# Projecting q, k and v of a first attention by halves, in three passes

## The chip, the cores and the metric

The kernel runs on one core of a Trainium2 chip. The metric is the device time of one execution in microseconds (us), lower is better. The profile is of one execution on the chip; its times are in us, those marked ns in nanoseconds. TensorE is PE in its rows (PEld are its weight loads), VectorE is DVE, ScalarE is ACT, GpSimd is POOL and SyncE is SP.

## The reference

Two transformer layers act on x of shape (4, 256, 256), 1,024 tokens in all. Each layer is an attention and a feed-forward part, each behind a layer norm with a shift and scale per batch. The change touches the first attention alone, which has 16 heads of 128 channels:

```python
q = _silu(x @ Wq)          # x: 1024 tokens x 256; each W: 256 x 2048
k = _silu(x @ Wk)
v = _silu(x @ Wv)
z = x @ Wz
```

q, k and v then pass a causal convolution of four taps along the sequence, q and k a rotary embedding and a norm; each token attends to itself and the three before it; the result is gated with silu(z), scaled and projected back to 256 columns. The later parts are a feed-forward layer whose weights are looked up in a table of 16 values, a second, full attention and a mixture of 32 experts.

## The kernel before

Everything is one hand-ordered program: each engine has its own instruction list, and semaphores order them. `project` multiplies one head's weights (two blocks of 128 x 128) with the 1,024 tokens of `h_t` in plain fp32; the profile shows each fp32 matmul as two records. The second attention uses `by_halves` instead: an operand is split into an upper part, rounded to the fp32r type by a copy, and a lower part, the rest; three single-pass products (lower times upper, upper times lower, upper times upper) add up in PSUM.

The first attention runs in turns, one per head. Turn h projects q, k, v and z of head h (work marked 1), finishes the attention of head h - 1 (marked 2) and transposes the gated result of head h - 2 (marked 3). `turns0` writes out turns 0, 1, 16 and 17 and loops over the pairs between; every engine runs the same turns with its own function `turn`. In one turn the engines do, each strictly in this order:

- TensorE: q; transpose of `rows_sb`; transposes of the gated result; k; S, the banded scores; v; z; transposes of v; sums of squares (`ssq`); the attention output o.
- ScalarE: silu and first tap of q; the copy into G; silu and first tap of k; the same of v; squares of q and k; silu of z; `v_tok`; the gate's tanh; squares of o (`sqo`).
- VectorE: gate mask `gm`; the other three taps of q's convolution (L1090); `ssq_s`; k's taps; the product A; cosine and sine parts (L1096, L1102); v's taps; the copy of the sums into `rows_sb` (L1139); the gate product `a0_g` (L1150).
- GpSimd: the norm's power, and the DMAs that add the rotary halves.
- SyncE: loads `b_all`, and the head after next's weights once z is done; it also fills two DRAM buffers for the experts.

The weights of a head lie in `wh[par]`, two buffers for even and odd heads. The table indices of the feed-forward part are loaded at the very start into `lut_w`; they are first used after the last turn.

Of the kernel before, what the change touches and what calls it, by code (L numbers as in the profile page):

```python
# [5 lines left out]
ALU = mybir.AluOpType  # L6
# [7 lines left out]
P = 128  # L14
# [45 lines left out]
def build(nc, a, out, b_rows, code_rows):  # L60
# [41 lines left out]
    with ctx:  # L102
# [42 lines left out]
        def carve(*sizes, base=0, of=arena):  # L145
# [8 lines left out]
        (uq, uk, uv, cq, ck, cv0, cv1, swq, swk, qr, kr, sqq, sqk, sz0, sz1, gm, A, v_tok, junk,  # L154
         rows_sb, gate, b_all, wh0, wh1) = carve(
            UW, UW, UW, T, T, T, T, T, T, T + PAD, T, T, T, T, T, BAND, BAND, T, T,
# [3 lines left out]
        cv, sz, wh = [cv0, cv1], [sz0, sz1], [wh0, wh1]  # L160
        wmod = [G[:, 0:KC * 6 * D], G[:, KC * 6 * D:2 * KC * 6 * D]]
# [6 lines left out]
        (wout,) = carve(H * D, base=3 * UW + 14 * T + PAD + 2 * BAND + P)  # L168
# [168 lines left out]
        def turns0(eng, turn):  # L337
            turn(0, 0, 0, (1,))
            turn(1, 0, 1, (1, 2))
            with eng.Fori(1, H // 2) as i:  # L340
                turn(2 * i, i, 0, (1, 2, 3))
                turn(2 * i + 1, i, 1, (1, 2, 3))
            turn(H, H // 2, 0, (2, 3))
            turn(H + 1, H // 2, 1, (3,))
# [18 lines left out]
        def _(sp):  # L363
# [8 lines left out]
            for par in range(2):  # L372
                sp.dma_start(wh[par], a["w_qkvz"][par]).then_inc(sg(f"a0_w{par}"), 16)
            sp.dma_start(lut_idx[:, 0:LPRE], a["idx_pre"]).then_inc(sg("in_idx"), 16)
            sp.dma_start(lut_idx[:, LPRE:LUTC - LPOST].rearrange("p (h c) -> p h c", c=LW),
                         a["idx"].rearrange("h p c -> p h c")).then_inc(sg("in_idx"), 16)
            sp.dma_start(lut_idx[:, LUTC - LPOST:LUTC], a["idx_post"]).then_inc(sg("in_idx"), 16)
# [24 lines left out]
            sp.wait_ge(sg("a0_z"), H)  # L402
            sp.wait_ge(sg("a0_gm"), H)
# [64 lines left out]
        def _(pe):  # L468
# [48 lines left out]
            def turn(h, hh, par, st):  # L517
                def w(j, k):
                    return wh[par][:, (j * KC + k) * P:(j * KC + k) * P + P]

                if 1 in st:
                    pe.wait_ge(sg(f"a0_w{par}"), 16 * (hh + 1))
# [4 lines left out]
                    project(slot(0), lambda k: w(0, k), P).then_inc(sg("a0_q"), 1)  # L527
# [13 lines left out]
                if 1 in st:  # L541
# [5 lines left out]
                    project(slot(1), lambda k: w(1, k), P).then_inc(sg("a0_k"), 1)  # L547
# [10 lines left out]
                if 1 in st:  # L558
                    pe.wait_ge(sg("a0_silu_q"), h + 1)
                    project(slot(0), lambda k: w(2, k), P).then_inc(sg("a0_v"), 1)  # L560
# [38 lines left out]

            turns0(pe, turn)  # L600
# [130 lines left out]
            pe.wait_ge(sg("in_lo"), KC)  # L731
# [112 lines left out]
        def _(act):  # L844
# [6 lines left out]

            def turn(h, hh, par, st):
# [30 lines left out]
                if 1 in st:  # L883
                    silu_and_tap(1, "k", ck)
                    silu_and_tap(2, "v", cv[par])
# [717 lines left out]
```

## Time and profile before

| what | us |
|---|---|
| median of 3 runs | 1256.71 |
| lowest and highest | 1248.58, 1257.54 |
| the profiled execution's own time | 1249.32 |
| its span | 1247.5 |
| TensorE busy in the span | 1091.8 (88%) |
| VectorE busy | 759.9 (61%) |
| ScalarE busy | 554.3 (44%) |
| GpSimd busy | 264.9 (21%) |

Busy time is a share of the whole span and averages over stages with different limits. In a stretch view each engine has its busy time with the count of its records; behind them stand the clock that was granted to TensorE (1.00 is 2.4 GHz, 0.50 is 1.2 GHz) and the DMA engines' share. A timeline row gives start and duration of a run of like instructions; what stands in brackets is how long the engine had idled before it and what released it. Records of a matmul overlap, so the pitch from start to start tells what one costs.

### The profile page before, as it was taken

The page shows a single profiled execution, that of the slowest core. Times are in us where ns is not written, and L with a number is a line of the kernel's source. Part 1 is how long each engine was busy: PE and PEld are TensorE (multiplying, and loading weights), DVE is VectorE, ACT ScalarE, POOL GpSimd, SP SyncE. Part 2 cuts the span into 40 slices and gives each one's busy share as a digit, 9 for nine tenths or more (in the row PEclk, how much of TensorE's full clock was granted, in tenths as well). Part 3 has the DMA queues.
Part 4 walks back from the last instruction along what each step waited for, and adds up shares of the span by engine and source line. Part 5 has one row for each costly group of instructions (what it writes and reads, how often), then busy time and mean ns, then how long its engine had stood idle before and what let it go on. Part 6 is the DMA issues. An engine that isn't in the chain of part 4 may idle for free.

```text
span 1247.5 us, 16995 instructions
## 1 busy us (share of the span) xinstructions
PE 1091.8 (88%) x5693; PEld 779.3 (62%) x5693; DVE 759.9 (61%) x1332; ACT 554.3 (44%) x1256; POOL 264.9 (21%) x228
## 2 busy tenths in 40 slices
PE   6989999999999979947977999999998967329996
PEld 4666667666766664423436999988985425128885
DVE  1497788878887858963136778787772034303344
ACT  1266767676766648920014555655551002002320
POOL 0032223222222220012002111111100000546660
PEclk9799999999999978978988999999998987759997
DMA  6055445643555330060001110111001000148854
GB/s 266 19 143 138 100 95 140 129 110 95 128 132 145 78 101 1 1 185 1 0 0 52 52 50 26 50 50 50 25 0 51 1 13 1 76 161 262 271 170 178
DMA packets 51349, 110.50 MB, mean 89 GB/s; under 512 B 7827, under 2 KB 30558, under 8 KB 50544
## 3 DMA queue, kind: packets, MB, share of 16 engines
q1 hardware_dynamic: 41584, 84.32, 20.9%
q0 software_dynamic: 9728, 25.72, 10.4%
q8 instruction: 20, 0.33, 0.1%
q14 instruction: 17, 0.14, 0.0%
HBM read 69.52 MB, written 27.89 MB: 78 GB/s over the span
## 4 chain that ended last, share of the span: by engine, by line
PE 41%; DVE 12%; issue 4%; POOL 3%; ACT 2%; DMA 1%; DVEq 0%; POOLq 0%; ACTq 0%; SPq 0%
PE psum L709 5%; PE psum L611 4%; PE psum L797 4%; PE psum L512 4%; PE psum L490 3%; PE psum L492 3%; PE psum L491 3%; PE psum L682 3%; PE psum L807 2%; DVE arena L1197 2%; POOL slot_rows L1514 2%; PE psum L628 2%; PE psum L249 1%; DVE lut_w L1197 1%; PE psum L786 1%
## 5 line engine op out<-in xcount | busy, mean ns | idle before, releaser
L1090 DVE SCALAR_TENSOR_TENSOR arena<-arena,par_in 128x1024 f32<-128x1024 f32 x144 | 184.7, 1284 | 52.5 <-ACT arena L870 38.3
L512 PE MATMUL psum<-h_t,arena 128*128 128x512 f32 x384 | 174.0, 597 | 0.0
L512 PEld LDWEIGHTS psum<-h_t,arena 128*128 128x128 f32 x384 | 69.3, 190 | 73.2 <-issue 73.2
L611 PE MATMUL psum<-G,arena 128*128 128x512 f32 x256 | 112.6, 602 | 2.7 <-DVE G L1289 1.5
L961 ACT ACTIVATE arena<-psum,small 128x256 f32<-128x256 f32 x128 | 59.2, 472 | 85.8 <-DVE small L1237 85.7
L611 PEld LDWEIGHTS psum<-G,arena 128*128 128x128 f32 x256 | 49.3, 193 | 64.8 <-issue 64.8
L1469 POOL TENSOR_TENSOR small<-small 128x16 f32<-128x16 f32 x16 | 46.8, 2928 | 199.5 <-DVE small L1116 199.5
L860 ACT ACTIVATE arena<-psum 128x1024 f32<-128x1024 f32 x48 | 49.3, 1026 | 83.4 <-PE psum L512 83.4
L490 PE MATMUL psum<-arena_r 128*128 128x256 f32 x256 | 77.7, 303 | 1.5 <-DVE arena_r L1262 1.5
L1475 POOL DMA_DIRECT2D arena<-arena x64 | 53.9, 983 | 117.4 <-DVE arena L1102 117.2
L286 POOL TENSOR_TENSOR small<-small 128x8 f32<-128x8 f32 x6 | 9.9, 1642 | 321.7 <-DVE small L277 305.7
L491 PE MATMUL psum<-arena_r 128*128 128x256 f32 x256 | 73.3, 286 | 0.0
L492 PE MATMUL psum<-arena_r 128*128 128x256 f32 x256 | 73.3, 286 | 0.0
L1522 POOL DMA_INDIRECT out_rows<-arena x64 | 62.7, 980 | 46.2 <-DVE arena L1382 24.0
L1491 POOL TENSOR_TENSOR arena_r<-arena,arena_r 128x512 fp32r<-128x512 f32 x16 | 21.2, 1325 | 217.0 <-ACT arena_r L972 217.0
L565 PEld LDWEIGHTS psum<-arena,h_t 128*128 128x128 f32 x512 | 59.7, 192 | 7.7 <-issue 7.7
L922 ACT ACTIVATE arena<-psum,small 128x128 f32<-128x128 f32 x128 | 44.9, 377 | 42.7 <-PE psum L596 42.7
L709 PE MATMUL psum<-arena,h_t 128*128 128x128 f32 x512 | 62.2, 275 | 0.0
L709 PEld LDWEIGHTS psum<-arena,h_t 128*128 128x128 f32 x512 | 60.7, 192 | 1.5 <-DVE arena_r L1255 0.2
L797 PE MATMUL psum<-arena 128*128 128x256 f32 x256 | 61.3, 383 | 0.0
L490 PE MATMUL psum<-lut_w_r,arena_r 128*128 128x512 f32 x128 | 51.4, 402 | 10.1 <-POOL arena_r L1491 10.1
L565 PE MATMUL psum<-arena,h_t 128*128 128x128 f32 x512 | 59.7, 274 | 0.0
(194 smaller groups left out, 2357.2 us busy)
## 6 DMA issues: line engine op xcount, KB each, us to landing
arena<-arena POOLq DMA_DIRECT2D x64, 256.0 KB, 7.6
arena<-in_w_moe SPq DMA_DIRECT2D x32, 384.0 KB, 3.8
slot_rows<-nowhere SPq DMA_DIRECT2D x16, 576.0 KB, 4.9
arena<-slot_rows SPq DMA_DIRECT2D x32, 288.0 KB, 3.9
arena<-in_w_qkvz SPq DMA_DIRECT2D x16, 512.0 KB, 3.8
arena<-b_rows SPq DMA_DIRECT2D x16, 512.0 KB, 9.0
arena<-in_qkv_codes SPq DMA_DIRECT2D x16, 384.0 KB, 3.2
arena<-in_qkv_scales SPq DMA_DIRECT2D x64, 96.0 KB, 3.0
```

Source lines behind the costliest of these rows:

```text
L490: nc.tensor.matmul(dst, w_l, x_h, start=start, stop=False, skip_group_check=True)
L491: nc.tensor.matmul(dst, w_h, x_l, start=False, stop=False, skip_group_check=True)
L492: return nc.tensor.matmul(dst, w_h, x_h, start=False, stop=stop, skip_group_check=True)
L512: i = nc.tensor.matmul(dst[0:rows, n * 512:n * 512 + 512], w(k), h_t[:, k * T + n * 512:k * T + n * 512 + 512], start=(k == 0), stop=(k == ...
L565: i = nc.tensor.matmul(slot(1)[:, t * P:t * P + P], h_t[:, k * T + t * P:k * T + t * P + P], w(3, k), start=(k == 0), stop=(k == KC - 1))
L611: i = nc.tensor.matmul(bank(2 * m + n), w[:, h * D + m * P:h * D + m * P + P], G[:, h * T + n * 512:h * T + n * 512 + 512], start=(h == 0) ...
L709: i = nc.tensor.matmul(slot(0)[:, t * P:t * P + P], h_t[:, k * T + t * P:k * T + t * P + P], w(2, k), start=(k == 0), stop=(k == KC - 1))
L797: i = nc.tensor.matmul(bank(2 + 2 * (e % 2) + j)[:, 0:CAP], we[e % WRING][:, k * D + j * P:k * D + j * P + P], xT[e % 2][:, k * CAP:(k + 1 ...
L961: e = nc.scalar.activation(prob[b % 2][:, i * S:i * S + S], bank(4 + b % 2)[:, i * S:i * S + S], ACT.Exp, bias=nmax[:, 2 * b + i:2 * b + i ...
L1090: nc.vector.scalar_tensor_tensor(by_batch(dst), by_batch(u[s])[:, :, j:j + S], par_in[:, bass.ds(M_CW + (w * H + h) * TAPS + j, 1)], by_ba ...
L1475: nc.gpsimd.dma_start(rot[s][to:to + 64, :], sw[s][of:of + 64, :], accum_op=ALU.add)\
L1522: nc.gpsimd.indirect_dma_start(out_rows, bass.IndirectOffsetOnAxis(place.bitcast(I32)[:, c:c + 1], 0), eo[e % RING][:, r * D:(r + 1) * D], ...
```

## The change

The q, k and v projections of the first attention go by halves; z stays fp32. The tokens are split once ahead of the first turn (`hh_h` by ScalarE, `hh_l` by VectorE, both laid over `lut_w`). Each head's q, k and v weights are split one turn ahead: ScalarE's `upper0` behind k's tap copies the upper part into `w_hi`, VectorE's `lower0` behind the copy of `rows_sb` writes the rest over the fp32 weights in place. `turns0` gets a mark 4 for that work, and turns 14 and 15 are now written out. The squares of o go into `v_tok` instead of a buffer of their own, which is dropped to make room, and the table indices are loaded behind the last z projection instead of at the start.

```diff
--- before.py
+++ after.py
@@ -151,13 +151,16 @@
             return v
 
         UW = B * (S + PAD)
-        (uq, uk, uv, cq, ck, cv0, cv1, swq, swk, qr, kr, sqq, sqk, sz0, sz1, gm, A, v_tok, junk,
+        (uq, uk, uv, cq, ck, cv0, cv1, swq, swk, qr, kr, sqq, sqk, sz0, sz1, gm, A, v_tok,
          rows_sb, gate, b_all, wh0, wh1) = carve(
-            UW, UW, UW, T, T, T, T, T, T, T + PAD, T, T, T, T, T, BAND, BAND, T, T,
+            UW, UW, UW, T, T, T, T, T, T, T + PAD, T, T, T, T, T, BAND, BAND, T,
             P, BAND, T, 4 * KC * P, 4 * KC * P)
         u, c_ = {"q": uq, "k": uk, "v": uv}, {"q": cq, "k": ck}
         sw, rot, sqr = {"q": swq, "k": swk}, {"q": qr[:, 0:T], "k": kr}, {"q": sqq, "k": sqk}
         cv, sz, wh = [cv0, cv1], [sz0, sz1], [wh0, wh1]
+        at_w = 3 * UW + 13 * T + PAD + 2 * BAND + P + BAND + T
+        wl0, _, wl1, _, w_hi0, w_hi1 = carve(QKV, KC * P, QKV, KC * P, QKV, QKV, base=at_w, of=arena_r)
+        w_lo, w_hi = [wl0, wl1], [w_hi0, w_hi1]
         wmod = [G[:, 0:KC * 6 * D], G[:, KC * 6 * D:2 * KC * 6 * D]]
         ba_sb = G[0:2 * H, 2 * KC * 6 * D:2 * KC * 6 * D + T]
 
@@ -165,7 +168,7 @@
         ln_c, ln_sq, ln_b, rb, gsb, hsb0, hsb1, lv0, lv1, lb0, lb1 = carve(
             KC * T, KC * T, T, T, T, T, T, (PAIRS - 1) * LC, (PAIRS - 1) * LC, LC, LC)
         lut_v, lut_b0 = [lv0, lv1], [lb0.bitcast(I32), lb1.bitcast(I32)]
-        (wout,) = carve(H * D, base=3 * UW + 14 * T + PAD + 2 * BAND + P)
+        (wout,) = carve(H * D, base=3 * UW + 13 * T + PAD + 2 * BAND + P)
         hsb = [hsb0, hsb1]
 
         QK = 2 * KC * P
@@ -335,11 +338,13 @@
 
 
         def turns0(eng, turn):
-            turn(0, 0, 0, (1,))
-            turn(1, 0, 1, (1, 2))
-            with eng.Fori(1, H // 2) as i:
-                turn(2 * i, i, 0, (1, 2, 3))
-                turn(2 * i + 1, i, 1, (1, 2, 3))
+            turn(0, 0, 0, (1, 4))
+            turn(1, 0, 1, (1, 2, 4))
+            with eng.Fori(1, H // 2 - 1) as i:
+                turn(2 * i, i, 0, (1, 2, 3, 4))
+                turn(2 * i + 1, i, 1, (1, 2, 3, 4))
+            turn(H - 2, H // 2 - 1, 0, (1, 2, 3, 4))
+            turn(H - 1, H // 2 - 1, 1, (1, 2, 3))
             turn(H, H // 2, 0, (2, 3))
             turn(H + 1, H // 2, 1, (3,))
 
@@ -371,10 +376,6 @@
             sp.dma_start(lut, a["lut"].broadcast_to([P, LUT])).then_inc(sg("in_lut"), 16)
             for par in range(2):
                 sp.dma_start(wh[par], a["w_qkvz"][par]).then_inc(sg(f"a0_w{par}"), 16)
-            sp.dma_start(lut_idx[:, 0:LPRE], a["idx_pre"]).then_inc(sg("in_idx"), 16)
-            sp.dma_start(lut_idx[:, LPRE:LUTC - LPOST].rearrange("p (h c) -> p h c", c=LW),
-                         a["idx"].rearrange("h p c -> p h c")).then_inc(sg("in_idx"), 16)
-            sp.dma_start(lut_idx[:, LUTC - LPOST:LUTC], a["idx_post"]).then_inc(sg("in_idx"), 16)
             sp.wait_ge(sg("ba_sb"), 1)
             sp.dma_start(b_rows, ba_sb[0:H, :]).then_inc(sg("b_rows"), 16)
             sp.wait_ge(sg("b_rows"), 16)
@@ -400,6 +401,10 @@
             turn(H - 2, H // 2 - 1, 0, False)
             turn(H - 1, H // 2 - 1, 1, False)
             sp.wait_ge(sg("a0_z"), H)
+            sp.dma_start(lut_idx[:, 0:LPRE], a["idx_pre"]).then_inc(sg("in_idx"), 16)
+            sp.dma_start(lut_idx[:, LPRE:LUTC - LPOST].rearrange("p (h c) -> p h c", c=LW),
+                         a["idx"].rearrange("h p c -> p h c")).then_inc(sg("in_idx"), 16)
+            sp.dma_start(lut_idx[:, LUTC - LPOST:LUTC], a["idx_post"]).then_inc(sg("in_idx"), 16)
             sp.wait_ge(sg("a0_gm"), H)
             sp.dma_start(wout, a["w_out"]).then_inc(sg("in_wout"), 16)
 
@@ -518,13 +523,21 @@
                 def w(j, k):
                     return wh[par][:, (j * KC + k) * P:(j * KC + k) * P + P]
 
-                if 1 in st:
-                    pe.wait_ge(sg(f"a0_w{par}"), 16 * (hh + 1))
+                def project0(dst, j):
+                    for n in range(2):
+                        for k in range(KC):
+                            w, c = slice((j * KC + k) * P, (j * KC + k) * P + P), slice(k * T + n * 512, k * T + n * 512 + 512)
+                            i = by_halves(dst[:, n * 512:n * 512 + 512], w_hi[par][:, w], w_lo[par][:, w], hh_h[:, c], hh_l[:, c],
+                                          k == 0, k == KC - 1)
+                    return i
+
+                if 1 in st:
+                    pe.wait_ge(sg("a0_w_lo"), h + 1)
                     if since(h, 1):
                         pe.wait_ge(sg("a0_silu_v"), h)
                     if since(h, 2):
                         pe.wait_ge(sg("a0_v_tok"), h - 1)
-                    project(slot(0), lambda k: w(0, k), P).then_inc(sg("a0_q"), 1)
+                    project0(slot(0), 0).then_inc(sg("a0_q"), 1)
                 if 2 in st:
 
                     pe.wait_ge(sg("a0_rows_sb"), h)
@@ -544,7 +557,7 @@
                     if since(h, 2):
                         pe.wait_ge(sg("a0_g"), h - 1)
                         pe.wait_ge(sg("a0_sqo"), h - 1)
-                    project(slot(1), lambda k: w(1, k), P).then_inc(sg("a0_k"), 1)
+                    project0(slot(1), 1).then_inc(sg("a0_k"), 1)
                 if 2 in st:
 
                     pe.wait_ge(sg("a0_rope_q"), 32 * h)
@@ -557,7 +570,7 @@
                     m.then_inc(sg("a0_S"), 1)
                 if 1 in st:
                     pe.wait_ge(sg("a0_silu_q"), h + 1)
-                    project(slot(0), lambda k: w(2, k), P).then_inc(sg("a0_v"), 1)
+                    project0(slot(0), 2).then_inc(sg("a0_v"), 1)
                 if 1 in st:
                     pe.wait_ge(sg("a0_silu_k"), h + 1)
                     for t in range(NT):
@@ -597,6 +610,7 @@
                                                  stop=True, skip_group_check=True)
                     m.then_inc(sg("a0_o"), 1)
 
+            pe.wait_ge(sg("in_lo"), KC)
             turns0(pe, turn)
 
             pe.wait_ge(sg("in_wout"), 16)
...
@@ -849,6 +863,12 @@
             act.wait_ge(sg("ba_ps"), 1)
             nc.scalar.activation(ba_sb, psum[0:2 * H, 4 * 512:4 * 512 + T], ACT.Copy).then_inc(sg("ba_sb"), 1)
 
+            def upper0(h, hh, par):
+                act.wait_ge(sg(f"a0_w{par}"), 16 * (hh + 1))
+                if since(h, 2):
+                    act.wait_ge(sg("a0_v"), h - 1)
+                nc.scalar.activation(w_hi[par], wh[par][:, 0:QKV], ACT.Copy).then_inc(sg("a0_w_hi"), 1)
+
             def turn(h, hh, par, st):
                 def cw(w, j):
                     return par_in[:, bass.ds(M_CW + (w * H + h) * TAPS + j, 1)]
@@ -882,6 +902,9 @@
                                          scale=par_in[:, bass.ds(M_NW + h - 2, 1)]).then_inc(sg("a0_gT_sb"), 1)
                 if 1 in st:
                     silu_and_tap(1, "k", ck)
+                if 4 in st:
+                    upper0(h + 1, hh + par, 1 - par)
+                if 1 in st:
                     silu_and_tap(2, "v", cv[par])
                     for s in "qk":
                         act.wait_ge(sg("a0_conv_" + s), 3 * h + 3)
@@ -895,7 +918,7 @@
                 if 2 in st:
                     act.wait_ge(sg("a0_vT"), h)
                     if since(h, 2):
-                        act.wait_ge(sg("a0_o"), h - 1)
+                        act.wait_ge(sg("a0_sqo"), h - 1)
                     act.wait_ge(sg("a0_rqk"), h)
                     for i in range(NT):
                         c = slice(i * P, i * P + P)
@@ -919,10 +942,14 @@
                         if i == NT // 2:
                             m.then_inc(sg("a0_sqo_lo"), 1)
                             act.wait_ge(sg("a0_g_hi"), h)
-                        m = nc.scalar.activation(junk[:, i * P:i * P + P], slot(1)[:, i * P:i * P + P], ACT.Square, scale=rqk[1 - par][:, i:i + 1],
+                        m = nc.scalar.activation(v_tok[:, i * P:i * P + P], slot(1)[:, i * P:i * P + P], ACT.Square, scale=rqk[1 - par][:, i:i + 1],
                                                  accum_out=ss_all[:, bass.ds((h - 1) * NT + i, 1)])
                     m.then_inc(sg("a0_sqo"), 1)
 
+            for k in range(KC):
+                act.wait_ge(*norm("n0", "out", k))
+                nc.scalar.activation(chunk(hh_h, k), chunk(h_t, k), ACT.Copy).then_inc(sg("in_hi"), 1)
+            upper0(0, 0, 0)
             turns0(act, turn)
             for c in range(LCH):
                 o, n = lut_cols(c)
@@ -1080,6 +1107,17 @@
                                     0.5, None, ALU.mult)\
                 .then_inc(sg("a_sb"), 1)
             dve.wait_ge(sg("in_par"), 16)
+            for k in range(KC):
+                dve.wait_ge(sg("in_hi"), k + 1)
+                nc.vector.tensor_tensor(chunk(hh_l, k), chunk(h_t, k), chunk(hh_h, k).bitcast(F32), ALU.subtract)\
+                    .then_inc(sg("in_lo"), 1)
+
+            def lower0(h, par):
+                dve.wait_ge(sg("a0_w_hi"), h + 1)
+                nc.vector.tensor_tensor(w_lo[par], wh[par][:, 0:QKV], w_hi[par].bitcast(F32), ALU.subtract)\
+                    .then_inc(sg("a0_w_lo"), 1)
+
+            lower0(0, 0)
 
             def turn(h, hh, par, st):
                 def conv(w, s, dst):
@@ -1137,6 +1175,8 @@
                     if since(h, 1):
                         dve.wait_ge(sg("a0_ssqT"), h)
                     nc.vector.tensor_copy(rows_sb[0:2 * NT, :], bank(7)[0:2 * NT, 0:P]).then_inc(sg("a0_rows_sb"), 1)
+                if 4 in st:
+                    lower0(h + 1, 1 - par)
                 if 2 in st:
 
                     dve.wait_ge(sg("a0_o"), h)
...
```

On VectorE, in the loop's first turn, the order before stood so between the last sine part and the next turn's gate mask (names in brackets are semaphores waited for; `ISA` rows set addresses in registers):

```order
L1102 TENSOR_TENSOR arena<-arena,cst 128x1024 [waits a0_rope_k]
L1090 ISA [waits a0_tap_v]
L1090 SCALAR_TENSOR_TENSOR arena<-arena,par_in 128x1024
L1090 ISA [waits a0_conv_v]
L1090 SCALAR_TENSOR_TENSOR arena<-arena,par_in 128x1024
L1090 ISA [waits a0_conv_v]
L1090 SCALAR_TENSOR_TENSOR arena<-arena,par_in 128x1024
L1139 COPY arena<-psum 16x128 [waits a0_ssqT,a0_ssq]
L1150 SCALAR_TENSOR_TENSOR arena<-psum,small,arena 128x128 [waits a0_silu_z,a0_o]
L1150 SCALAR_TENSOR_TENSOR arena<-psum,small,arena 128x128 x3
```

The same engine and place in the changed kernel (L1117 is `lower0`, L1177 the copy of `rows_sb`, L1190 the gate product):

```order
L1128 SCALAR_TENSOR_TENSOR arena<-arena,par_in 128x1024
L1177 COPY arena<-psum 16x128 [waits a0_ssqT,a0_ssq]
L1116 REGISTER_ALU
L1117 TENSOR_TENSOR arena_r<-arena,arena_r 128x768 [waits a0_w_hi]
L1190 SCALAR_TENSOR_TENSOR arena<-psum,small,arena 128x128 [waits a0_silu_z,a0_o]
L1190 SCALAR_TENSOR_TENSOR arena<-psum,small,arena 128x128 x3
```

One subtraction of 768 columns has come in between the copy and the gate product; nothing else on VectorE changed places inside a turn.

On TensorE, between the attention output of one turn (L592, L596) and the q projection of the next (L512), before:

```order
L592 MATMUL psum<-arena 128x128 x2
L596 MATMUL psum<-arena 3x128
L512 MATMUL psum<-h_t,arena 128x512 [waits a0_v_tok,a0_silu_v,a0_w1]
L512 MATMUL psum<-h_t,arena 128x512 x3
L533 MATMUL psum<-cst,arena 128x128 [waits a0_ssq_s,a0_rows_sb]
```

And in the changed kernel (L605, L609 are the attention output; L495 to L497 the three products of `by_halves`, which repeat to twelve):

```order
L605 MATMUL psum<-arena 128x128 x2
L609 MATMUL psum<-arena 3x128
L535 REGISTER_ALU
L495 MATMUL psum<-lut_w_r,arena_r 128x512 [waits a0_v_tok,a0_silu_v,a0_w_lo]
L496 MATMUL psum<-lut_w_r,arena_r 128x512
L497 MATMUL psum<-lut_w_r,arena_r 128x512
```

The order of the products among TensorE's other work is the same; the q projection now waits for the semaphore of `lower0` where it waited for the weights' DMA.

## Rows read from the trace of the kernel before

**Rows 1.** Stretches, by engine: busy us (count); then granted clock, DMA share, GB/s.

```profile
95.13:422.30 327.17, 327.17 (x1887) 223.44 (x1886) 271.90 (x338) 229.02 (x546) 81.66 (x65) 1.00 0.49 117
...
220.96:246.13 25.17, 25.17 (x146) 17.19 (x146) 20.91 (x26) 17.62 (x42) 6.28 (x5) 1.00 0.50 117
```

**Rows 2.** Timeline, turn 7: start us, us, engine, line, operation, idle before.

```profile
220.96 3.70 PE L512 MATMUL psum<-h_t,arena 128*128 128x512 f32 x8
...
224.78 1.03 ACT L860 ACTIVATE arena<-psum 128x1024 f32<-128x1024 f32 x1 [0.70 <-PE psum L512]
...
227.27 1.29 DVE L1090 SCALAR_TENSOR_TENSOR arena<-arena,par_in 128x1024 f32<-128x1024 f32 x1 [2.27 <-ACT arena L870]
...
230.29 1.15 ACT L870 ACTIVATE arena<-arena,par_in 128x1024 f32<-128x1024 f32 x1
...
231.61 4.14 DVE L1090 SCALAR_TENSOR_TENSOR arena<-arena,par_in 128x1024 f32<-128x1024 f32 x3
...
234.35 1.03 ACT L860 ACTIVATE arena<-psum 128x1024 f32<-128x1024 f32 x1 [2.92 <-PE psum L512]
...
245.49 0.27 DVE L1139 COPY arena<-psum 16x128 f32<-16x128 f32 x1
```

**Rows 3.** Timeline of TensorE: single by-halves matmuls of the second attention.

```profile
662.67 0.63 PE L492 MATMUL psum<-lut_w_r,arena_r 128*128 128x512 f32 x1
...
663.95 0.63 PE L492 MATMUL psum<-lut_w_r,arena_r 128*128 128x512 f32 x1
...
750.27 0.40 PE L490 MATMUL psum<-lut_w_r,arena_r 128*128 128x512 f32 x1
...
752.14 0.39 PE L492 MATMUL psum<-lut_w_r,arena_r 128*128 128x512 f32 x1
```

**Rows 4.** By form, VectorE and ScalarE, early second attention: count | busy, mean ns.

```profile
L1262 DVE TENSOR_TENSOR arena_r<-psum,arena_r 128x512 fp32r<-128x512 f32 x5 | 3.3, 683 | 0.0
...
L1225 DVE TENSOR_TENSOR lut_w_r<-h_t,lut_w_r 128x1024 fp32r<-128x1024 f32 x2 | 2.4, 1222 | 0.0
...
L998 ACT ACTIVATE lut_w_r<-h_t 128x1024 fp32r<-128x1024 f32 x2 | 2.1, 1058 | 14.2 <-DVE h_t L297 14.2
```

**Rows 5.** Timeline of the start, heads 0 and 1.

```profile
47.68 1.01 ACT L850 ACTIVATE G<-psum 32x1024 f32<-32x1024 f32 x1 [30.00 <-PE psum L499]
...
49.36 10.57 PE L512 MATMUL psum<-h_t,arena 128*128 128x512 f32 x24
...
71.56 0.27 DVE L1139 COPY arena<-psum 16x128 f32<-16x128 f32 x1
...
73.03 3.93 DVE L1090 SCALAR_TENSOR_TENSOR arena<-arena,par_in 128x1024 f32<-128x1024 f32 x3
...
91.42 0.28 DVE L1139 COPY arena<-psum 16x128 f32<-16x128 f32 x1
```

**Rows 6.** Timeline of the stage's end.

```profile
449.20 1.12 DVE L1150 SCALAR_TENSOR_TENSOR arena<-psum,small,arena 128x128 f32<-128x128 f32 x4 [0.51 <-ACT arena L922]
...
451.56 0.33 SPq L404 DMA_DIRECT2D arena<-in_w_out  x1
...
472.63 29.80 PE L611 MATMUL psum<-G,arena 128*128 128x512 f32 x64 [1.25 <-issue]
```

**Rows 7.** Holes of TensorE and the clock behind them: timeline rows, and two stretches.

```profile
77.84 2.04 PE L556 MATMUL psum<-arena 128*128 128x131 f32 x16 [2.19 <-DMA arena<-arena]
...
78.00:82.00 4.00, 4.00 (x22) 2.80 (x22) 3.93 (x4) 0.00 (x0) 2.06 (x1) 1.00 0.00 0
...
449.50:452.00 2.50, 1.61 (x8) 1.57 (x8) 2.07 (x6) 1.07 (x7) 0.34 (x1) 0.51 0.07 13
...
450.39 1.97 PE L539 MATMUL psum<-cst,arena 128*128 128x128 f32 x8 [2.59 <-DVE arena L1150]
...
940.08 0.66 PE L682 MATMUL psum<-cst,arena 128*128 128x128 f32 x4 [1.70 <-DVE arena L1246]
...
941.40 1.11 PE L682 MATMUL psum<-cst,arena 128*128 128x128 f32 x4 [0.66 <-DVE arena L1246]
```

More of the change, by code:

```diff
@@ L729, in turn1 @@
                     m.then_inc(sg("a1_o"), 1)
-            pe.wait_ge(sg("in_lo"), KC)
+            pe.wait_ge(sg("in_lo"), 2 * KC)
             turns1(pe, turn1)
@@ L1223, in _ @@
             for k in range(KC):
-                dve.wait_ge(sg("in_hi"), k + 1)
+                dve.wait_ge(sg("in_hi"), KC + k + 1)
                 nc.vector.tensor_tensor(chunk(hh_l, k), chunk(h_t, k), chunk(hh_h, k).bitcast(F32), ALU.subtract)\
```

## The prediction

> **What bounds the kernel now.** I read the stretches first. From the first q projection of the steady loop to the last (13 turns, 95.13 to 422.30) TensorE is busy for every microsecond, 327.17 of 327.17, at granted clock 1.00, while VectorE has 271.90 and ScalarE 229.02; one turn, 220.96 to 246.13, takes 25.17 us, with VectorE busy for 20.91 of it [rows 1]. So TensorE sets the pace of this stage, and a shorter TensorE stream alone would shorten it. The timeline of one turn shows how near the next bound is [rows 2]. A q projection starts at 220.96; ScalarE reads it (silu) 3.82 us later, at 224.78; after its tap VectorE starts the q convolution at 227.27, 2.49 us on. From there VectorE has work until the copy of `rows_sb` at 245.49, 18.22 us later, and ends it at 245.76. The next q projection starts at 246.13. At present nothing ties it to the copy.
>
> **The change, part by part.** *TensorE.* A projection is now 4 fp32 matmuls, shown as 8 records; q, k and v are three of them per head. Eight records at a pitch of 0.4275 us (3.82 less the last one's 0.40 of latency) are 3.42 us. By halves it is 12 single matmuls of 512 columns, whose pitch in the second attention is 1.87/8 = 0.234 us [rows 3], so 2.80 us. That is 0.62 us less per projection, 1.86 per turn, 29.8 over 16 heads. TensorE's own turn falls to 25.17 - 1.86 = 23.31 us.
>
> *The new wait.* The q projection of head h+1 waits for `lower0(h+1)`, and this stands on VectorE behind the `rows_sb` copy of turn h, that is, behind everything that hangs on the q projection of turn h. This closes a ring: q projection, silu, tap, VectorE's whole turn, lower0, next q projection. Its length: 3.82 - 0.62 = 3.20 to the silu; 2.49 to the convolution; 18.22 to the copy, less 0 to 0.1, because the k convolution at 231.61 now starts just when the tap at 230.29 (1.15 long) lets it, and that tap comes 1.24 earlier while the q convolution comes only 0.62 earlier [rows 2]; 0.2 for the copy; lower0; 0.15 for the handover to TensorE. A VectorE subtraction of this form takes 1.22 us for 1,024 columns and 0.68 for 512 [rows 4], so 0.95 for 768. Sum: 3.20 + 2.49 + 18.22 + 0.2 + 0.95 + 0.15 = 25.21 us, less half of that 0.1, which I take as 25.15 (25.0 to 25.3, by the handover and the copy). Against 25.17 the turn gains nothing: 13 turns give -0.2 us (-2.2 to +1.7). TensorE then idles about 1.84 us in each turn, always between the attention outputs and the q projection. Behind the waiting q projection stand the transposes of the norm, k, S, v and z; all of them slide with it.
>
> *ScalarE.* `upper0` adds a copy of 768 columns; one of 1,024 takes 1.06 us [rows 4], so it is 0.8 by the columns and 1.06 at most. It stands after k's tap, where ScalarE waits 2.92 us for the v projection [rows 2]; that wait shrinks to some 2.3 and still hides it. The wait of `v_tok` on `a0_sqo` instead of `a0_o` is met one turn early, since the buffer of the squares is now `v_tok`. VectorE's gate product (`a0_g`) moves behind lower0; its 2.3 us and the gate mask's 1.24 end 2 us before the next q convolution and cost nothing while the ring is 25 us long.
>
> *The start.* Before, q of head 0 starts at 49.36, right behind ScalarE's copy that ends at 48.69 [rows 5]. Now ScalarE copies two halves of h_t (1.06 each) and one weight block, VectorE subtracts twice (1.22, the second from about 51.1) and once 0.95, so q(0) starts at 53.2: +3.85. VectorE's turn 0 begins 3.85 - 0.62 = 3.2 later, its copy comes at 71.56 + 3.2 = 74.8, and q(1) at 76.0. VectorE's turn 1 begins 5.69 us later, at 81.7, where it began at 73.03. It then runs without the gaps it had (18.39 us to 91.42, some 0.9 of it waiting) in 17.5 [rows 5], so q(2) starts at 99.2 + 1.25 = 100.5 instead of 95.13: **+5.35 us** before the loop is reached.
>
> *The end.* Turn 14 is now written out rather than looped; its nine convolution steps run without the loop's 0.07 each: -0.66. In turn 15 there is no lower0, TensorE and VectorE are both done about 1.9 us sooner after q(15), and the gate product that ended at 450.32 moves with them: -1.9. The index loads now go out behind the last z, and w_out behind them. The w_out load went out at 451.56 and is used at 472.63 [rows 6]; 21 us cover its 2 MB and what is left of the indices. Moving them out of the first 20 us frees no one, since TensorE there follows its own queue: 0.
>
> Sum with the clock left alone: 5.35 - 0.2 - 0.66 - 1.9 = **+2.6 us**.
>
> **The clock.** The 1.84 us hole per turn is the unknown. A hole of 2.19 us before S left the clock at 1.00 [rows 7]. A hole of 2.59 us behind the same attention outputs left it at 0.51, and one of 1.70 us in the second attention, with 0.66 behind it, was followed by four transposes in 1.11 us where four had taken 0.66. The case of 1.70 us and the one with the same neighbours (outputs before the hole) both went down, so I take it that the clock falls to 1.2 GHz in part of the turns. A by-halves matmul has a pitch of 0.427 us there [rows 3], so a whole q projection loses 12 x 0.193 = 2.3 us; the bounds per turn are 0 and 2.3, and since a spell need not last for the whole projection (8 slow ones would cost 8 x 0.193 = 1.5), I take 1.45 for a turn that is hit, and 8 of the 14 turns from q(2) on: +11.6. At the start TensorE idles 3.85 us before q(0) and some 7 before q(1): 1.7 + 2.0 = +3.7. All of it lies on the ring.
>
> The Trainium skill (TensorE: Matmul & The Clock Gate, section "Why this matters for your kernels") names only idle gaps longer than these 1.84 us as a cause of a drop. By that rule the steady turns would stay at 2.4 GHz and the time would be that of the first rival; the trace does not agree at 1.70 us.
>
> Sum: 2.6 + 3.7 + 11.6 = +17.9 us on the profiled execution's 1249.3, so 1267. That execution is near the lowest of the three runs, and their median lies 7.4 above it. I add half of this, since other runs may fall on either side: **1271 us**, against a like-for-like 1253 before (+1.4%).
>
> **The rivals.** *First, the clock stays up.* For it: the 2.19 us hole, with dense projections around it. Against it: the 1.70 us one. Then 1253 + 2.6 = 1256; with a ring of 25.0, 1254.
>
> *Second, it falls in nearly every turn.* For it: the holes come at one place of each turn, behind sparse outputs. 14 x 1.7 + 5.3 + 2.6 = +31.7, 1284.
>
> *Third, the other side: lower0 is never late.* If VectorE's turn had slack, TensorE would set a turn of 23.31 us: 13 x 1.84 less, 1253 + 2.8 - 24 = 1232. VectorE is busy for only 20.91 + 0.95 = 21.9 us of it, which speaks for it; but its busy time is not what matters, the ring is. It decides only below 23.31 us, and the rows give 25.15 without a free term of 1.8.
>
> **How the numbers follow.** Forecast (falls in part) 0.48; clock up 0.33; falls nearly always 0.14; lower0 never late 0.05. Range 1252 to 1285: it leaves out the last case and the outer ends of the first and second rival. About 1% is what a measurement here can tell from no change. Slower by over 1%: most of the forecast (1267 and more) and the second rival, 0.55. Within 1%: the rest of the forecast and the first rival, 0.40. Faster by over 1%: 0.05.
>
> **What would show it.** In the profile after: a turn of about 25.15 us in which the first by-halves matmul follows a VectorE subtraction with some 1.8 us of idle time put down to it; q(2) near 100.5; granted clock under 1.00 in the stretch 100 to 420. If the granted clock stands at 1.00 there, the clock term falls away; if TensorE is fully busy, the ring was wrong; if TensorE idles before the o or ssq products, ScalarE's queue is the bound that I hid. Turns nearer 27 us throughout would be the second rival.

## The result and the profile after

The changed kernel takes 1258.58 us (median of 20 runs, 1251.62 to 1262.25) against 1250.78 for the kernel before (20 runs). The medians are 7.8 us apart; over all runs the ratio is put at 1.0045, 95% interval 1.0025 to 1.0065, which is slower by 0.45% or 5.6 us (3.1 to 8.1), within the 1% that was called "no change". The forecast was 1271 and slower by 1.4%, or 18 us. The direction held; the size was two to three times too large. The profiled execution took 1252.23 us, 2.9 above the profiled one of before, and is near the quickest of its runs.

Stretches of the kernel after: from the q projection of head 2 to that of head 15, one turn, and the one turn in which the clock fell (us, busy us with count for TensorE, its weight loads, VectorE, ScalarE and GpSimd; then granted clock, DMA share, GB/s):

```profile
102.58:427.13 324.55, 306.47 (x2041) 252.37 (x2042) 279.60 (x352) 239.19 (x554) 94.31 (x65) 0.99 0.49 117
227.21:252.18 24.97, 23.47 (x157) 19.33 (x158) 21.59 (x28) 18.58 (x45) 7.26 (x5) 1.00 0.49 119
302.04:328.47 26.43, 25.02 (x158) 20.47 (x158) 21.43 (x28) 18.36 (x44) 7.25 (x5) 0.94 0.46 110
```

TensorE, which was busy in all of this stage [rows 1], now has 23.47 us of work in a turn of 24.97, and the stage is 2.6 us shorter than the 327.17 of before. Of its 13 turns 11 last 24.88 to 24.98, one 26.43, and the written-out one at its end 23.90. What TensorE waits for from 100 to 430 us is one thing (us in total, times, longest):

```profile
PE psum L495 <- DVE arena_r L1117: 19.6, 14, 1.5
```

The timeline of turn 7 shows the ring, and answers to [rows 2]:

```profile
227.21 0.50 PE L495 MATMUL psum<-lut_w_r,arena_r 128*128 128x512 f32 x1 [1.41 <-DVE arena_r L1117]
...
232.88 1.28 DVE L1128 SCALAR_TENSOR_TENSOR arena<-arena,par_in 128x1024 f32<-128x1024 f32 x1 [2.50 <-ACT arena L890]
...
250.91 0.27 DVE L1177 COPY arena<-psum 16x128 f32<-16x128 f32 x1
...
251.11 0.94 DVE L1117 TENSOR_TENSOR arena_r<-arena,arena_r 128x768 fp32r<-128x768 f32 x1
...
252.18 0.49 PE L495 MATMUL psum<-lut_w_r,arena_r 128*128 128x512 f32 x1 [1.51 <-DVE arena_r L1117]
```

From q to VectorE's convolution of it 5.67 us, to the copy of `rows_sb` 18.03, to `lower0` (L1117) 0.20, and to the next q 1.07. The start answers to [rows 5], and the end to [rows 6]:

```profile
52.74 0.76 PE L495 MATMUL psum<-lut_w_r,arena_r 128*128 128x512 f32 x1 [3.70 <-DVE arena_r L1117]
...
75.96 0.27 DVE L1177 COPY arena<-psum 16x128 f32<-16x128 f32 x1
...
77.16 0.79 PE L495 MATMUL psum<-lut_w_r,arena_r 128*128 128x512 f32 x1 [6.41 <-DVE arena_r L1117]
...
83.93 3.93 DVE L1128 SCALAR_TENSOR_TENSOR arena<-arena,par_in 128x1024 f32<-128x1024 f32 x3 [5.67 <-ACT arena L890]
...
453.20 1.97 PE L552 MATMUL psum<-cst,arena 128*128 128x128 f32 x8 [2.49 <-DVE arena L1190]
...
454.33 0.33 SPq L409 DMA_DIRECT2D arena<-in_w_out  x1
...
475.44 2.90 PE L625 MATMUL psum<-G,arena 128*128 128x512 f32 x3 [1.25 <-issue]
```

The time can now be added up between the two profiled executions. q(2) starts 7.45 us later (102.58 for 95.13). The stage to q(15) gives back 2.62, of which the clock fall took 1.5: without it, 4.1. From q(15) to the transposes that wait for the last gate product (450.39 before, 453.20 now) it is 26.07 us for 28.09, another 2.0. So the output projection starts 2.81 later (475.44 for 472.63), and the whole is 2.9 longer. The load of w_out, 21.1 us ahead of that projection, delayed nothing.

### The profile page after: what moved, and what is told of

The parts are those of the page before. It is cut to its first block, busy times and chain, and to the rows that moved or that the text cites. A ratio compares the mean times of both kernels' runs of the same rounds, so it can differ in the third digit from the quotient of the medians.

```text
span 1250.4 us, 17351 instructions
## 1 busy us (share of the span) xinstructions
PE 1067.0 (85%) x5885; PEld 816.8 (65%) x5885; DVE 773.1 (62%) x1350; ACT 569.6 (46%) x1274; POOL 279.5 (22%) x228
## 4 chain that ended last, share of the span: by engine, by line
PE 40%; DVE 12%; issue 4%; POOL 3%; ACT 2%; DMA 1%; DVEq 0%; POOLq 0%; ACTq 0%; SPq 0%
PE psum L723 4%; PE psum L625 4%; PE psum L811 4%; PE psum L517 4%; PE psum L495 3%; PE psum L497 3%; PE psum L496 3%; PE psum L696 2%; PE psum L821 2%; DVE arena L1237 2%; POOL slot_rows L1554 2%; PE psum L642 2%; PE psum L252 1%; DVE lut_w L1237 1%; PE psum L800 1%
## 5 line engine op out<-in xcount | busy, mean ns | idle before, releaser
L495 PE MATMUL psum<-lut_w_r,arena_r 128*128 128x512 f32 x320 | 133.7, 418 | 39.9 <-DVE arena_r L1117 29.7
L496 PE MATMUL psum<-lut_w_r,arena_r 128*128 128x512 f32 x320 | 129.0, 403 | 0.0
L497 PE MATMUL psum<-lut_w_r,arena_r 128*128 128x512 f32 x320 | 128.3, 401 | 0.0
L1509 POOL TENSOR_TENSOR small<-small 128x16 f32<-128x16 f32 x16 | 61.4, 3839 | 202.1 <-DVE small L1154 202.1
L495 PEld LDWEIGHTS psum<-lut_w_r,arena_r 128*128 128x128 f32 x320 | 61.9, 193 | 57.7 <-issue 20.9
L495 PE MATMUL psum<-arena_r 128*128 128x256 f32 x256 | 77.7, 304 | 1.5 <-DVE arena_r L1302 1.5
L497 PE MATMUL psum<-arena_r 128*128 128x256 f32 x256 | 73.4, 287 | 0.0
L497 PEld LDWEIGHTS psum<-lut_w_r,arena_r 128*128 128x128 f32 x320 | 61.8, 193 | 14.9
L496 PEld LDWEIGHTS psum<-lut_w_r,arena_r 128*128 128x128 f32 x320 | 62.1, 194 | 11.2
L723 PE MATMUL psum<-arena,h_t 128*128 128x128 f32 x512 | 62.2, 275 | 0.0
L723 PEld LDWEIGHTS psum<-arena,h_t 128*128 128x128 f32 x512 | 60.7, 192 | 1.5 <-DVE arena_r L1295 0.2
```

The costliest lines, as they stand in the source:

```text
L495: nc.tensor.matmul(dst, w_l, x_h, start=start, stop=False, skip_group_check=True)
L496: nc.tensor.matmul(dst, w_h, x_l, start=False, stop=False, skip_group_check=True)
L497: return nc.tensor.matmul(dst, w_h, x_h, start=False, stop=stop, skip_group_check=True)
L723: i = nc.tensor.matmul(slot(0)[:, t * P:t * P + P], h_t[:, k * T + t * P:k * T + t * P + P], w(2, k), start=(k == 0), stop=(k == KC - 1))
L1509: nc.gpsimd.tensor_tensor(rqk[1 - par], ssq_s, neg_half, ALU.pow).then_inc(sg("a0_rqk"), 1)
```

## Experiments

Each ratio is taken against runs of the kernel before on the same chip. The changed kernel itself ran once more beside experiments 1 to 4. Experiments 5 to 7, and experiment 8, ran later on two other chips without it, so what is said there of the changed kernel compares across chips, on which the kernel before had medians of 1253.25, 1251.27 and 1254.20 us. q(n) is the start of head n's q projection.

**1. The changed kernel again.** 

> The changed kernel once more, unchanged, beside the others, to see whether the one clock fall in fourteen steady turns of its first profiled execution was typical. If the clock term is what was mis-sized by much, this profile again shows few full turns near 26.4 us and most near 24.93 us, and a median near 1258. If the first profile was an exception and my 8 of 14 turns is the usual case, it shows 6 to 10 turns longer than 26 us and a profiled time near 1262 or above. With 6.4 us between the first profiled execution and the median of its runs, some 4 or 5 turns at 26.4 us are what I look for.

1258.31 us, ratio 1.0038 (1.0014 to 1.0063). This profile took 1263.26, 11.0 above the first, and its q projections show where from: four turns of 26.42 to 26.53 us instead of one. One of them (start, us, engine, line; idle time before it in brackets):

```profile
183.16 0.50 PE L495 MATMUL psum<-lut_w_r,arena_r 128*128 128x512 f32 x1 [1.44 <-DVE arena_r L1117]
...
209.66 0.50 PE L495 MATMUL psum<-lut_w_r,arena_r 128*128 128x512 f32 x1 [1.50 <-DVE arena_r L1117]
```

Four is what I had looked for. From q(2) to q(15) this makes 4.6 us for three more falls. Another 4.3 us come ahead of everything that the change touches; 2.7 of them are in the small matmuls of the modulation, which took 5.42 us at a granted clock of 0.99 in the first profile, and here 8.14 at 0.64:

```profile
13.97 8.14 PE L480 MATMUL psum<-small,G 128*128 128x4 f32 x48
```

The rest (2.1) lies behind the stage. So the spread between executions is mostly TensorE's clock, and it is not the change's alone. The 20 runs above say the same: the four quickest (1251.62 to 1253.10 us) have a mean granted clock of 0.921 to 0.924, the other sixteen one of 0.913 to 0.918. A single profile against the median of other runs says little about a change.

**2. The subtraction ahead of v's convolution.**

```
                     sin_part("k")
+                if 4 in st:
+                    lower0(h + 1, 1 - par)
+                if 1 in st:
                     conv(2, "v", cv[par])
 ...
-                if 4 in st:
-                    lower0(h + 1, 1 - par)
```

> VectorE's subtraction for the next head's q and k weights is moved from behind its convolution of v to ahead of it; nothing else changes. Theory (the ring through VectorE's whole turn sets 24.93 us): the q projection of the next head no longer waits for the end of VectorE's turn, the hole of 1.41 to 1.55 us closes, and a turn falls to TensorE's own 23.4 to 23.6 us: 13 x 1.35 = 17 to 20 us less than the changed kernel, so 1238 to 1241 median, with the clock at 1.00 in the turns. Rival A (something else, a bank or ScalarE, sets the turn): the turn stays within 0.2 us of 24.93 and the time within 2 us. Rival B (VectorE's copy of rows and v's chain, 0.94 us later now, becomes the bound): the turn lands at 24.2 or above, 8 us or less gained.

1244.00 us, ratio 0.9938 (0.9913 to 0.9962): 14 us quicker than the changed kernel by moving one VectorE instruction of 0.95 us. The ring through `lower0` is thereby shown. A turn is 24.21 us, neither 23.5 nor 24.93: the turn is my rival B's, and the gain of 14 us lies between its 8 or less and the theory's 17 to 20. By the profiles 9.2 us of it are in the 13 turns (falls left aside), 4.0 between q(0) and q(1), and the rest is the falls, of which this profile has none. One turn, and what TensorE still waits for in it:

```profile
223.73:247.94 24.21, 23.72 (x158) 19.27 (x158) 21.51 (x28) 18.36 (x43) 7.26 (x5) 1.00 0.52 122
```
```profile
227.29 1.09 PE L552 MATMUL psum<-cst,arena 128*128 128x128 f32 x8 [0.39 <-DVE arena L1191]
```

The transposes of the gated result wait for VectorE's gate product (L1191), and k's projection stands behind them: the ring now closes one step further on, through the same VectorE turn.

**3. TensorE's hole filled.**

```
+                        for _ in range(6):
+                            nc.tensor.matmul(bank(0), hh_h[:, 0:P], hh_h[:, 0:512], start=True, stop=True,
+                                             skip_group_check=True)
+                    pe.wait_ge(sg("a0_w_lo"), h + 1)
```

> Six dummy products of 512 columns are added to TensorE ahead of its wait for the next head's subtracted weights, in every head from the third on; what they write is overwritten. They fill 1.4 us of the hole and leave VectorE's work as it is. Ring theory: a turn stays at 24.9 us, since TensorE only did nothing there. Clock theory (it is the hole before the q projection from which the clock falls in some turns): no turn of the profile shows half clock, and the median moves to the quick end of the changed kernel's runs, 1251 to 1253, some 5 us below it. Rival: the falls don't come from the hole (or are no part of the turns): the time stays at 1258 within 1.5, or rises if the dummies are late and push the q projection.

```profile
101.80:424.80 323.00, 323.00 (x2119) 264.33 (x2118) 280.04 (x353) 239.83 (x558) 94.30 (x65) 1.00 0.49 118
```

(This stretch of 323 us spans the thirteen turns; q(2) is at 102.17 and q(15) at 425.64.) The steps from q to q are 24.84 to 24.93 us in all looped turns: 1.4 us of TensorE work more in each cost nothing, so TensorE does not set the changed kernel's turn. The six products fill the hole to its end, though: TensorE is busy for all of the stretch and here is as long as the ring, and in the written-out turn, whose hole was only 0.57 us, they cost 0.85 (24.75 for 23.90). None of the 13 turns shows half clock. The median is 1256.15, ratio 1.0033 (1.001 to 1.0056), 2.2 below the changed kernel where I expected 5; the two intervals overlap, so this gain is seen in the profile's turns and not shown by the times. In this profile the part behind q(15) took 827.7 us, 4.4 longer than in the first of the changed kernel. Over the ten profiles of this document that part lies between 823.3 and 828.1 us, with 825.2 for the kernel before, so this is its spread between executions; what makes the spread is open.

**4. The start.** ScalarE splits the tokens and the first weights ahead of its copy of the b and a projections, VectorE subtracts ahead of the second modulation.

```
+            for k in range(KC):
+                act.wait_ge(*norm("n0", "out", k))
+                nc.scalar.activation(chunk(hh_h, k), chunk(h_t, k), ACT.Copy).then_inc(sg("in_hi"), 1)
+            upper0(0, 0, 0)
             act.wait_ge(sg("ba_ps"), 1)
             nc.scalar.activation(ba_sb, psum[0:2 * H, 4 * 512:4 * 512 + T], ACT.Copy).then_inc(sg("ba_sb"), 1)
 ...
-            modulation(1)
 ...
+            modulation(1)
```

> At the start alone: ScalarE's splitting of the tokens and the upper half of the first weights move ahead of its copy of the b and a projections, and VectorE's subtraction for them moves ahead of the second modulation. Theory (the first q projection at 52.74 us, after a wait of 3.70 us, is late because its split operands queue behind other work on the two engines): it starts at about 49.1 us, in full clock since the hole before it closes, and the whole moves 3.7 to 5.4 us earlier: 1253 to 1255 median, the turns unchanged at 24.93 us. Rival (the start is bound by the arrival of the norm or by the modulation, which now comes later on VectorE and delays the first tap): the second q projection stays within 1 us of 77.16 and the time within 1.5 us of the changed kernel.

```profile
49.05 0.50 PE L495 MATMUL psum<-lut_w_r,arena_r 128*128 128x512 f32 x1
```
```profile
71.82 0.79 PE L495 MATMUL psum<-lut_w_r,arena_r 128*128 128x512 f32 x1 [6.41 <-DVE arena_r L1111]
```

1250.97 us, ratio 0.9988 (0.9961 to 1.0015), 7.3 below the changed kernel, a little more than expected. The profile shows 3.7 of waiting, and q(0) without its hole runs at full clock, so that q(0) to q(1) is 22.8 us and not 24.4. The 1.7 us that I had set for q(0)'s clock are this difference. Behind q(1) half clock lasts longer than in the changed kernel and takes back 0.9 (26.33 us to q(2) for 25.42), so q(2) comes 4.4 earlier. The other 3 us of the medians' distance do not show in the turns (this profile has one fall, like the first of the changed kernel) and lie within the two intervals.

**5. Both.** The edits of experiments 2 and 4 together.

> The early start (experiment 4) and the subtraction ahead of v's convolution (experiment 2) together. In the first's profile the second q projection began 5.3 us earlier; in the second's a turn took 24.21 us for 24.93. Theory (the two act in different places and add up): turns of 24.21 us, no half clock in them, and about 1244 - 6 = 1237 to 1240 us median. Rival (the early start is given back, since in the second kernel the first turns already run closer to TensorE's own pace and don't wait as long for the second and third q): 1241 to 1244.

1238.09 us (6 runs), ratio 0.9882 (0.9857 to 0.9907): the two add up, and this version beats the kernel before by 1.2% and, by the two ratios, the changed one by 1.6%. From q(2) to q(15) the clock stays up, although the first of these turns lasts 26.24 us, since S waits 2.74 us there for a transfer that adds the rotary halves. The stage, a stretch around that wait, and the matmul behind it:

```profile
97.25:413.14 315.89, 307.80 (x2042) 250.62 (x2042) 279.45 (x350) 238.69 (x559) 94.29 (x65) 1.00 0.51 121
103.80:112.00 8.20, 5.46 (x35) 4.65 (x34) 7.60 (x8) 3.20 (x4) 3.90 (x1) 1.00 0.09 29
```
```profile
106.84 2.04 PE L569 MATMUL psum<-arena 128*128 128x131 f32 x16 [2.74 <-DMA arena<-arena]
```

The hole ahead of q(1) is 2.39 us both here and in experiment 2. Here q(1) ran at full clock, there mostly at half clock. First this version, then experiment 2, each with the hole and the stretch from q(1) on:

```profile
72.48 0.50 PE L495 MATMUL psum<-lut_w_r,arena_r 128*128 128x512 f32 x1 [2.39 <-DVE arena_r L1111]
```
```profile
72.48:75.30 2.82, 2.82 (x12) 2.17 (x12) 2.75 (x3) 0.00 (x0) 1.25 (x2) 1.00 0.95 224
```
```profile
78.15 0.50 PE L495 MATMUL psum<-lut_w_r,arena_r 128*128 128x512 f32 x1 [2.39 <-DVE arena_r L1117]
```
```profile
78.15:81.00 2.85, 2.85 (x8) 2.23 (x9) 2.78 (x3) 0.00 (x0) 1.26 (x2) 0.57 0.65 191
```

So the length of a hole alone does not decide the clock behind it.

**6. The subtraction on GpSimd.** With the start of experiment 4, `lower0` goes out of VectorE's turn altogether.

```
+                if h < H - 1:
+                    pool.wait_ge(sg("a0_w_hi"), h + 2)
+                    nc.gpsimd.tensor_tensor(w_lo[1 - par], wh[1 - par][:, 0:QKV], w_hi[1 - par].bitcast(F32), ALU.subtract)\
+                        .then_inc(sg("a0_w_lo"), 1)
                 if 2 in st:
                     pool.wait_ge(sg("a0_ssq_s"), h)
```

> The subtraction of each next head's lower half goes from VectorE to GpSimd, which stands idle till the power operation of the turn, with the early start of experiment 4. GpSimd takes 1.30 us for 128 x 512 of the same kind in the second attention, so about 1.95 us for 128 x 768. Theory (with 0.94 us less on VectorE's part, the ring through k is 23.3 us and TensorE's own work, 23.7 to 23.8 us busy in a turn, is the bound): turns of 23.5 to 23.9 us, TensorE without holes, and 1232 to 1236 us median. Rival (GpSimd's operation is long or slows VectorE while both read, or it holds up the power operation and the transfers queued behind it on GpSimd): a turn stays at 24.2 or above and the time at 1238 or more.

1244.69 us, ratio 0.9942 (0.9923 to 0.9961): 6.6 slower than experiment 5, where I expected a gain. A turn is 24.98 us, for 24.21. The two lines (count, min/median/max ns, first and last start, form), GpSimd's subtraction and VectorE's convolution steps:

```profile
L1504 POOL TENSOR_TENSOR arena_r<-arena,arena_r x15: 1832/1840/2792, 54.7 to 401.4; 128x768 fp32r<-128x768 f32 x15
```
```profile
L1129 DVE SCALAR_TENSOR_TENSOR arena<-arena,par_in x144: 1267/1284/2915, 51.3 to 437.0; 128x1024 f32<-128x1024 f32 x144
```

GpSimd's operation has the expected length, but the convolution step that runs beside it takes up to 2.92 us for 1.28 (in experiment 5 the longest is 1.31). VectorE saves 0.95 us per turn and loses about 1.6 to GpSimd's 1.84, and it is VectorE's turn that the ring counts: TensorE's wait for the gate product, 0.39 us in the turn shown for experiment 2, is 0.9 on average here, and no wait for GpSimd's subtraction shows.

**7. VectorE's cost doubled.** In every head one more VectorE operation of the subtraction's size ahead of it.

```
+                nc.vector.tensor_tensor(wh[par][:, 0:QKV], wh[par][:, 0:QKV], wh[par][:, 0:QKV], ALU.max).then_inc(sg("a0_twice"), 1)
+                dve.wait_ge(sg("a0_twice"), h + 1)
```

> In every head VectorE does one more operation of the subtraction's size just ahead of it (the maximum of the weights with themselves, 128 x 768, about 0.94 us, and 0.06 us or so for its semaphore): nothing of the result changes. Ring theory (the ring runs through this operation): a turn becomes 24.93 + 0.95 to 1.05 = 25.9 to 26.0 us and the hole ahead of q 2.4 to 2.5 us. Rival (VectorE has slack elsewhere, the ring takes it up): the turn grows by under 0.3 us. On the clock: if it is the length of the hole from which the clock falls, as my forecast had it (2.19 us left it up once, 2.59 came with half clock), now at least half of the 14 steady turns are 1.4 to 1.6 us longer still; if the hole's length hardly matters, 1 to 4 of 14 as before, and the median is 1258 + 14 = 1272.

1289.96 us (4 runs), ratio 1.0312 (1.0281 to 1.0343), far above 1272. The holes have the expected length, and all 13 turns from q(2) to q(15) hold a fall; two successive q projections, and a stretch of two turns:

```profile
188.78 0.50 PE L495 MATMUL psum<-lut_w_r,arena_r 128*128 128x512 f32 x1 [2.41 <-DVE arena_r L1119]
...
216.28 0.50 PE L495 MATMUL psum<-lut_w_r,arena_r 128*128 128x512 f32 x1 [2.49 <-DVE arena_r L1119]
```
```profile
188.78:243.71 54.93, 50.05 (x315) 40.92 (x315) 44.95 (x57) 36.93 (x86) 14.51 (x10) 0.94 0.45 107
```

A looped turn is 27.3 to 27.5 us: 24.93, the 1.0 that was added, and 1.5 of clock. The ring and the dependence on the hole both come out. Half clock also follows the hole of 1.57 us ahead of q(15), a length at which most turns of the changed kernel kept full clock.

**8. A third of it.** The same with `[:, 0:256]`, to have the hole that the forecast had assumed.

> As in the doubling before it, but the added operation of VectorE has a third of the size (128 x 256, about 0.35 us and its semaphore), so that the hole ahead of q is about 1.84 us, the length that my forecast gave to the changed kernel, between the 1.41 to 1.51 us with half clock in 1 and 4 of 14 turns and the 2.4 to 2.5 us with half clock in all. Ring: the turn becomes 24.93 + 0.4 = 25.3 us where the clock stays up. If the forecast's chance of a fall was right for its hole, 6 to 12 of the 14 turns are some 1.5 us longer (about 26.8 us), and the median is 1258.3 + 5.6 + 6 to 15 = 1270 to 1279. If the clock holds for holes under 2 us, 0 to 4 turns are longer and the median is 1262 to 1266.

```profile
211.58 0.49 PE L495 MATMUL psum<-lut_w_r,arena_r 128*128 128x512 f32 x1 [1.95 <-DVE arena_r L1119]
...
238.41 0.50 PE L495 MATMUL psum<-lut_w_r,arena_r 128*128 128x512 f32 x1 [1.87 <-DVE arena_r L1119]
```
```profile
211.58:238.41 26.83, 24.96 (x158) 20.43 (x158) 21.86 (x29) 18.49 (x43) 7.25 (x5) 0.94 0.44 107
```

1272.77 us (4 runs), ratio 1.0140 (1.0121 to 1.0159). Turns without a fall last 25.34 to 25.42, as expected; 9 of the 13 hold one and last 26.6 to 27.0 (25.9 in the written-out turn). The falls stand behind holes of 1.86 to 1.95 us, 9 of 11 such; behind two of 1.69 and 1.71 us the clock stayed up. The forecast's share and this run agree: at the hole that it assumed, most turns fall.

The holes of the steady turns and the turns with half clock, from the profiles:

| version | hole before q, us | turns with a fall, of 13 | median, us |
|---|---|---|---|
| filled (3) | none | 0 | 1256.15 |
| subtraction earlier (2), both (5), GpSimd (6) | none | 0, 0, 0 | 1244.00, 1238.09, 1244.69 |
| changed kernel, two profiles | 1.41 to 1.55 | 1, 4 | 1258.58, 1258.31 |
| early start (4) | 1.42 to 1.54 | 1 | 1250.97 |
| a third more (8) | 1.69 to 1.95 (11 of them 1.86 or more) | 9 | 1272.77 |
| doubled (7) | 2.38 to 2.53 | 13 | 1289.96 |

## Why the forecast had the direction and not the size

**The ring: right.** VectorE's subtraction behind the copy of `rows_sb` ties each q projection to the one before it. It was forecast at 25.15 us and is 24.93: q to the convolution 5.67 (forecast 5.69), VectorE's turn to the copy 18.03 (18.17), from the copy on 1.27 (1.30) in the turn shown. Experiments 2, 3 and 7 show it from three sides: the instruction earlier, TensorE's work more for nothing, VectorE's work more at its full price. "TensorE sets the pace" before and "the ring does" after differ by 0.24 us in 25, which is why 1.7 us less TensorE work in a turn (25.17 to 23.47) saved almost nothing. The twelve looped turns give 12 x 0.24 = 2.9 of the 4.1 us, the written-out one the other 1.3. Of that, 0.66 is the convolution steps without the loop, as forecast (18.03 us from the convolution to the copy became 17.37), and 0.33 more lies between q and its convolution (5.34 for 5.67), which was not forecast. The sum had -0.2 and -0.66 for these turns, 3.2 us too slow, and the looped turns alone lie outside its -2.2 to +1.7 for the ring: the ring of 24.93 us is just under its stated 25.0 to 25.3.

**The start: right but for its size.** +5.35 with the clock left alone and +3.7 for the clock make 9.05; q(2) came 7.45 later. q(0) was 3.4 later (forecast 3.85), and its clock cost the 1.7 that experiment 4 gives back. VectorE's turn 1 began 10.9 us later (83.93 for 73.03), where the forecast had 8.7 (81.7 for 73.03) and with its 3.7 of clock 12.4. Half clock in q(1) was the smaller item: q(1) to its convolution took 6.77 us, 1.1 more than in a steady turn, where I had put 2.0. From there to q(2) it was 18.65 us, for 18.8 forecast.

**The end: right.** -1.9 forecast, -2.0 measured, and w_out was covered as said.

**The clock in the turns: this step failed.** The forecast said "1.45 for a turn that is hit, and 8 of the 14 turns from q(2) on: +11.6". The price of a fall was right (1.5 us). The count was not: 1 and 4 of 13 turns in two profiles of the changed kernel, 1.5 to 6 us. Experiment 8 makes visible how the steps behind it failed. Where the hole really has the length that I had put in, 9 of 13 turns fall, which is the forecast's share; the changed kernel's hole is 1.41 to 1.55 us and not 1.84, since it is the difference of two sums, a ring 0.2 us shorter than forecast and a TensorE turn 0.2 us longer (23.47 for 23.31). Errors of under 1% in each made one of a fifth in the hole, and the number of falls changes most steeply just there. I had taken the share from two rows of other stages and carried it as if a few tenths in the hole's length did not matter. One of these rows I also read too simply: the four transposes right behind the hole of 1.70 us still took 0.66 us at a granted clock of 1.00 (940.08 to 940.74), and only those behind the next idle 0.66 us ran at 0.50. A range over the hole would, by the table, have shown some 2 to 13 us for this term.

**The base: a second, smaller miss.** I added 3.7 us, half the distance of the profiled execution from the median of three runs. Over 20 runs the kernel before has a median of 1250.78, 1.5 above that execution. With the measured terms, 7.45 - 4.1 - 2.0 + 1.5 to 6 is +2.8 to +7.3 us; the ratio of the runs says +5.6 (3.1 to 8.1), and the medians are 7.8 apart. So the terms account for the change within its interval. How often the clock fell in the runs that were not profiled is not shown.

**The rivals.** "The clock stays up" (1256) was nearer than the forecast, though the clock did not stay up: it fell in few turns. "Falls in nearly every turn" is what a hole of 2.4 us brings (experiment 7), and "lower0 is never late" is what experiment 2 makes of it, at 24.21 and not at 23.31 us, since the ring then closes behind the gate product. The rule of the Trainium skill that was cited (TensorE: Matmul & The Clock Gate, section "Why this matters for your kernels") names only longer gaps as a cause. The runs do not agree: gaps of 1.86 to 1.95 us ahead of q were followed by half clock in 9 of 11 turns. Nor does the length of the gap alone decide: 2.74 us ahead of S left the clock up in experiment 5, and 2.39 us ahead of q(1) did so there and not in experiment 2. For the hole ahead of the steady q, its length is not separated from the turn's length, which grew with it, and what else decides is open.

## What to carry to other kernels

Before work is taken off the engine that sets the pace, write down the ring through the next engine, instruction by instruction, and ask where in that engine's queue the new helper operation will stand: here its place was worth 14 us and its duration 0.95. A hole that a change opens on TensorE is the difference of two large sums; give the clock term a range over the hole's length, or close the hole, since a few tenths of a microsecond decided between 1 and 9 falls. And compare medians of many runs, with the start of the program looked at apart, before a profile is set against a median.

## What the runs showed of the hardware

- Half clock in the q projection behind TensorE's hole came in a share of the turns that rises with the hole (the table of experiment 8), and with it the matmuls of 512 columns go at 0.427 us instead of 0.234, about 1.5 us a time. Elsewhere in the turn a longer hole (2.74 us ahead of S, experiment 5) left the clock at 1.00.
- The 48 small matmuls at the program's start (128 x 4) take 5.42 us at a granted clock of 0.99 or 8.14 at 0.64, from one execution to the next of the same kernel.
- GpSimd's subtraction of 128 x 768 (1.84 us) stretches a VectorE convolution step beside it from 1.28 us to as much as 2.92.
